# A change to the latent attention stage: values in two 64-column halves, sums in 32-column quarters, a third probability buffer

## Chip, cores and metric

The kernel runs on one core of a Trainium2 chip. The metric is the device time of one launch in microseconds. The kernel is a chain of eight stages (a state-space block, a mixture of experts, a rotary attention, the experts again, the latent attention, a second mixture of experts, a grouped attention, the experts once more); the change touches only the latent attention.

## What is computed

Input `x` is (4, 512, 256). The stage in question adds to `x` the output of `_L1_attn_a_ref` on the layer-normed `x`. Its latent half, cut to what matters:

```
q_mid = rmsnorm(hidden_states @ q_a_w.T, q_a_ln_w)
q = (q_mid @ q_b_w.T).reshape(b, s, H, D_Q).transpose(0, 2, 1, 3)
...
qf = jnp.concatenate([q_nope, q_pe], -1)
kf = jnp.concatenate([k_nope, k_pe], -1)
scores = jnp.einsum('bhqd,bhkd->bhqk', qf, kf) * scale
probs = jax.nn.softmax(scores.astype(jnp.float32), axis=-1).astype(dt)
ctx = jnp.einsum('bhqk,bhkd->bhqd', probs, v)
main_out = ctx.transpose(0, 2, 1, 3).reshape(b, s, H * D_V) @ o_w.T
```

There are 4 batches, 16 heads and 512 tokens. The kernel composes the key and value up-projections with the query and output weights, so that keys and values of all heads are the same 64 latent numbers a token (plus 64 rotary ones for the keys).

## The kernel before

The stage is the function `latent()`. Heads are worked on in 32 pairs (4 batches of 8; `g` counts pairs, `i` is the head within one). A pair has four units, one for each tile of 128 keys (`kt`). One list `events` sets the order of the work, and each engine (PE, ACT, DVE, POOL, and the queue of DMA issues) walks through the same list and takes from it what is its own; a semaphore counter of each engine tells the others how far it is. So the order on an engine is the order of the list, and an instruction that waits holds all that stands behind it on its engine.

In unit `n` the list has: `s` of the first head (three float32r matmuls at L226 to L228 in `mm3` and one that adds the negative maximum, L1932), what `slots` puts at place 0, `s` of the second head, place 1, then `pv` (L1935, probabilities times values) of the unit before for the first head, place 2, `pv` for the second, place 3. A pair has 16 places. The places hold, for the next pair `n`: `kc`, `qc`, `qn` (copies of keys and queries on DVE) at 0, `kp` and `qp` (rope inputs; ACT copies, DMA swaps, POOL combines at L1787, L1789, L1791) at 3 and 11, `mx` (L1921 on PE and the reduction L2128 on DVE) at 4 to 11, `kl` and `ql` (the low halves, L2112) at 5 and 7, `bias` at 13; and for the pair before: `norm` (DVE, L2133 to L2144) at 12, and after every second pair `out` (output projection into DVE's `main`) at 1 and 2. The first pair of a batch has its places otherwise. The side matmuls share two PSUM banks in turn (`slot`), so each waits until the last but one has been read.

The scores of a unit are in two PSUM banks, the exponential (L1987, ACT) writes `PB[n % 2]`, and `pv` reads it as a plain float32 matmul. Its stationary operand is a window of 128 columns of `VT`: 64 columns of values and 64 of ones, the other way round for the second head, so that one matmul gives both the context and the sum of probabilities, head by head in bank 6 and bank 7. `sums` (L1996, L1997, ACT) copies four pieces of 64 partitions, `norm` transposes the sums, takes reciprocals, spreads them and multiplies.

## Time and profile before

| | us |
|---|---|
| time, median of 3 | 4568.15 (4564.28 to 4572.83) |
| profiled execution, its own time | 4568.12 |
| its span | 4566.3 |
| granted TensorE clock, mean | 0.912 |
| PE busy over the span | 3840.6 (84%) |
| DVE busy | 2580.8 (57%) |
| the stage's pairs (1845 to 2730 us) | 885 |

The span runs from the first to the last instruction of the profiled execution. Busy times of engines overlap; which of them sets the end is read from the waits and from the chain of work that ended last. Matmul ends are modelled, so the spacing of starts tells more than durations.

### The profile page before, as it was taken

The numbers are of one execution on the slowest core, as the hardware profiler recorded it, in microseconds if no ns is written. First come the engines' busy times: TensorE is split into PE (matmuls) and PEld (weight loads), VectorE is DVE, ScalarE is ACT, GpSimd is POOL, SyncE is SP. The second block draws the span as 40 slices with busy tenths as digits, with TensorE's granted clock in tenths as the row PEclk, the third lists the DMA queues.
The fourth block names the chain that finished last, engine by engine and source line by source line (L and its number), as shares of the span: only waits on it lengthen the run. The fifth ranks groups of instructions, "written<-read, shape, count | busy, mean of one in ns | idle before, by whom it ended". The sixth has DMA issues, their size and how long they took to land.

```text
span 4566.3 us, 44420 instructions
## 1 busy us (share of the span) xinstructions
PE 3840.6 (84%) x15840; PEld 2548.4 (56%) x15840; DVE 2580.8 (57%) x4324; ACT 1687.5 (37%) x2807; POOL 1353.1 (30%) x1074
## 2 busy tenths in 40 slices
PE   6869778887978883888889887999878888879999
PEld 4647544435844432555555555788744444457887
DVE  5645366654456652678686765433356766655333
ACT  2433256653235540232323223222245555522222
POOL 3234322214320102333323314444322221143442
PEclk8989889988989976999999998999989999979999
DMA  1010000001000002101000101000000000010000
GB/s 56 1 37 5 29 1 1 1 1 41 1 22 5 5 5 80 28 16 26 18 24 17 26 16 58 18 27 9 16 1 1 1 1 1 1 58 21 25 13 19
DMA packets 32760, 83.27 MB, mean 18 GB/s; under 512 B 6304, under 2 KB 7456, under 8 KB 32288
## 3 DMA queue, kind: packets, MB, share of 16 engines
q1 hardware_dynamic: 32544, 80.44, 5.7%
q8 instruction: 130, 2.13, 0.2%
q14 instruction: 86, 0.70, 0.0%
HBM read 59.44 MB, written 4.19 MB: 14 GB/s over the span
## 4 chain that ended last, share of the span: by engine, by line
PE 54%; DVE 22%; ACT 5%; POOL 3%; issue 2%; DMA 1%; SPq 1%; DVEq 0%; POOLq 0%; ACTq 0%
PE ps L226 11%; PE ps L227 10%; PE ps L228 10%; DVE max_cols L1149 7%; PE ps L1096 5%; PE ps L1935 3%; PE ps L1090 2%; PE ps L296 2%; DVE q_lo L2112 2%; DVE max_cols L2128 2%; PE ps L1081 2%; ACT probs L1126 1%; PE ps L1086 1%; PE ps L800 1%; PE ps L1077 1%
## 5 line engine op out<-in xcount | busy, mean ns | idle before, releaser
L1149 DVE TENSOR_REDUCE max_cols<-ps 128x1 fp32r<-128x512 f32 x1024 | 635.6, 680 | 284.9 <-PE ps L1081 284.1
L1126 ACT ACTIVATE probs<-ps 128x512 f32<-128x512 f32 x1024 | 546.1, 603 | 256.5 <-PE ps L1090 164.6
L754 POOL TENSOR_TENSOR h_lo<-h,h_hi 128x512 fp32r<-128x512 f32 x304 | 392.5, 1291 | 816.6 <-ACT h_hi L834 816.6
L911 DVE TENSOR_TENSOR gated<-silu,ps 128x512 f32<-128x512 f32 x288 | 197.9, 687 | 689.1 <-PE ps L228 665.7
L828 ACT ACTIVATE silu<-ps 128x512 f32<-128x512 f32 x304 | 181.9, 598 | 928.0 <-PE ps L228 927.9
L226 PE MATMUL ps<-xn_hi,w_hi 128*128 128x512 f32 x1216 | 479.5, 394 | 0.0
L227 PE MATMUL ps<-xn_lo,w_hi 128*128 128x512 f32 x1216 | 476.0, 391 | 0.0
L228 PE MATMUL ps<-xn_hi,w_lo 128*128 128x512 f32 x1216 | 475.8, 391 | 0.0
L1096 PE MATMUL ps<-probs,v_aug 128*32 128x512 f32 x2048 | 310.3, 683 | 0.0
L330 POOL CAST o_hi<-o_scaled 128x512 fp32r<-128x512 f32 x64 | 39.1, 612 | 910.1 <-DVE o_scaled L1171 910.1
L1935 PE MATMUL ps<-probs,v_tok 128*128 128x512 f32 x512 | 263.5, 611 | 2.7 <-ACT denominators L1997 2.7
L226 PEld LDWEIGHTS ps<-xn_hi,w_hi 128*128 128x128 f32 x1216 | 231.0, 190 | 49.8 <-issue 1.0
L227 PEld LDWEIGHTS ps<-xn_lo,w_hi 128*128 128x128 f32 x1216 | 230.4, 189 | 49.6 <-issue 1.4
L228 PEld LDWEIGHTS ps<-xn_hi,w_lo 128*128 128x128 f32 x1216 | 230.0, 189 | 48.6
L226 PE MATMUL ps<-h_hi,w_hi 128*128 128x512 f32 x608 | 249.4, 410 | 1.2 <-POOL h_lo L754 1.2
L1090 PE MATMUL ps<-q_stack,k_alone 128*128 128x512 f32 x512 | 213.9, 440 | 31.3 <-ACT probs L1126 29.1
L227 PE MATMUL ps<-h_lo,w_hi 128*128 128x512 f32 x608 | 239.7, 394 | 0.0
L228 PE MATMUL ps<-h_hi,w_lo 128*128 128x512 f32 x608 | 239.6, 394 | 0.0
L1090 PE MATMUL ps<-q_stack,k_stack 64*128 64x512 f32 x512 | 198.8, 485 | 43.3 <-ACT probs L1126 41.2
L1987 ACT ACTIVATE probs<-ps 128x1024 f32<-128x1024 f32 x128 | 131.2, 1025 | 279.1 <-PE ps L1932 278.9
L1081 PE MATMUL ps<-k_alone,q_stack 128*128 128x512 f32 x512 | 201.7, 432 | 37.8 <-ACT q_stack L1115 23.7
L2128 DVE TENSOR_REDUCE max_cols<-ps 128x1 fp32r<-128x512 f32 x256 | 169.2, 682 | 89.6 <-PE ps L1921 89.3
(460 smaller groups left out, 7896.1 us busy)
## 6 DMA issues: line engine op xcount, KB each, us to landing
raw<-in_w_ffn SPq DMA_DIRECT2D x76, 448.0 KB, 3.3
raw<-raw SPq DMA_DIRECT2D x256, 64.0 KB, 2.0
composed_inputs<-in_m_latent SPq DMA_DIRECT2D x1, 5120.0 KB, 15.5
raw<-in_w_mamba SPq DMA_DIRECT2D x8, 448.0 KB, 5.9
raw<-in_w_latent SPq DMA_DIRECT2D x5, 448.0 KB, 16.8
x<-in_x SPq DMA_DIRECT2D x4, 512.0 KB, 6.2
gated_pattern<-gated SPq DMA_DIRECT2D x4, 512.0 KB, 3.1
raw<-gated_pattern SPq DMA_DIRECT2D x4, 512.0 KB, 4.3
```

What stands on the lines that cost most here:

```text
L226: nc.tensor.matmul(psum, wh, xh, start=start, stop=False)
L227: nc.tensor.matmul(psum, wh, xl, start=False, stop=False)
L228: return nc.tensor.matmul(psum, wl, xh, start=False, stop=stop)
L754: nc.gpsimd.tensor_tensor(HL[:, b % 3, :], hb[:, b % 2, :], HH[:, b % 3, :].bitcast(F32), ALU.subtract).then_inc(G.sem, G.step((s, ev)))
L911: nc.vector.tensor_tensor(ga if routed(i) else hb[:, i % 2, :], sg[:, i % 2, :], bank[2 + i % 2], ALU.mult).then_inc(V.sem, V.step((s, "ga ...
L1081: last = nc.tensor.matmul(self.psum(ev), self.q_rows(g, h)[:, q * P:(q + 1) * P], self.k_rows(g, h), start=True, stop=True)
L1090: last = nc.tensor.matmul(self.scores(self.step_no(g, kt, h)), self.k_rows(g, h)[:, kt * P:(kt + 1) * P], self.q_rows(g, h), start=True, s ...
L1096: last = nc.tensor.matmul(bank[6][32 * h:32 * h + 32, :], self.VA[:, (g // self.G4) % 2, kt, self.khead((g % self.G4) * 4 + h), :], self.P ...
L1126: nc.scalar.activation(self.PB[:, n % 8, :], self.scores(n), ACT.Exp, scale=self.scale).then_inc(A.sem, A.step((s, ("exp", n))))
L1149: nc.vector.tensor_reduce(self.MB[:, self.tile_of(g, h) % 2, q, col:col + 1], self.psum(ev), op=ALU.max, axis=AX.X, negate=True).then_inc( ...
L1935: last = nc.tensor.matmul(bank[6 + i], VT[:, (g // HP) % 2, kt, 64 - 64 * i:192 - 64 * i], PB[:, (g * QT + kt) % 2, i, :], start=kt == 0, ...
L2128: nc.vector.tensor_reduce(MB[:, q, 32 * i:32 * i + 1], bank[slot(ev)], op=ALU.max, axis=AX.X, negate=True).then_inc(V.sem, V.step((s, ev)))
```

## The change

The values of both heads come out side by side in one bank: two matmuls of 64 columns, into partitions 0 to 63 and 64 to 127 of bank 6. `VT` loses its ones. The sums are matmuls of their own, `add`, after every second key tile: four matmuls with 32 columns of ones, each into 32 partitions of bank 7; a quarter is one head and the even or the odd key tiles. So that both tiles' probabilities are still there, `PB` has three buffers. Both heads' `pv` (and `add`, `sums`) now stand together ahead of places 2 and 3. The copies of `sums` are two of 128 partitions. The transpose of the sums is an event of its own (`turn`, place 7), ACT then swaps neighbouring quarters in four small copies (`swap`, place 10), and `norm` adds the two parts before the reciprocal.

```diff
-            VT = alloc("v_tok", [P, 2, QT, 192])
-            PB = alloc("probs", [P, 2, 2, L])
+            VT = alloc("v_tok", [P, 2, QT, 64])
+            PB = alloc("probs", [P, 3, 2, L])
+            sums = alloc("sums", [P, 2, L // 32])
...
+                put(n, 7, ("turn", g))
+                put(n, 10, ("swap", g))
                 put(n, 12, ("norm", g))
...
-                for i in (0, 1):
-                    if n:
-                        events.append(("pv",) + units[n - 1] + (i,))
-                        if i and units[n - 1][1] == QT - 1:
-                            events.append(("sums", units[n - 1][0]))
-                    events += at[2 + i]
+                if n:
+                    events.append(("pv",) + units[n - 1])
+                    if units[n - 1][1] % 2:
+                        events.append(("add",) + units[n - 1])
+                    if units[n - 1][1] == QT - 1:
+                        events.append(("sums", units[n - 1][0]))
+                events += at[2] + at[3]
...
                     elif kind == "pv":
-                        g, kt, i = ev[1:]
-                        last = nc.tensor.matmul(bank[6 + i], VT[:, (g // HP) % 2, kt, 64 - 64 * i:192 - 64 * i],
-                                                PB[:, (g * QT + kt) % 2, i, :], start=kt == 0, stop=kt == QT - 1)
+                        g, kt = ev[1:]
+                        for i in (0, 1):
+                            last = nc.tensor.matmul(bank[6][64 * i:64 * i + 64, :], VT[:, (g // HP) % 2, kt, :],
+                                                    PB[:, (g * QT + kt) % 3, i, :], start=kt == 0, stop=kt == QT - 1)
+                    elif kind == "add":
+                        g, kt = ev[1:]
+                        for q in range(4):
+                            i, back = q // 2, 1 - q % 2
+                            last = nc.tensor.matmul(bank[7][32 * q:32 * q + 32, :], ones[:, 0:32],
+                                                    PB[:, (g * QT + kt - back) % 3, i, :], start=kt == 1, stop=kt == QT - 1)
...
-                        act.wait_ge(PE.sem, PE.at((s, ("pv", g, QT - 1, 1))))
+                        act.wait_ge(PE.sem, PE.at((s, ("add", g, QT - 1))))
                         if g:
                             act.wait_ge(V.sem, V.at((s, ("norm", g - 1))))
-                        for i in (0, 1):
-                            r, r2 = slice(64 * i, 64 * i + 64), slice(64 - 64 * i, 128 - 64 * i)
-                            nc.scalar.activation(ctx_[r, :], bank[6 + i][r, :], ACT.Copy).then_inc(A.sem, A.step())
-                            nc.scalar.activation(DN[r, :], bank[6 + i][r2, :], ACT.Copy).then_inc(A.sem, A.step((s, ev)))
+                        nc.scalar.activation(ctx_, bank[6], ACT.Copy).then_inc(A.sem, A.step())
+                        nc.scalar.activation(DN, bank[7], ACT.Copy).then_inc(A.sem, A.step((s, ev)))
+                    elif kind == "swap":
+                        act.wait_ge(V.sem, V.at((s, ("turn", ev[1]))))
+                        for q in range(4):
+                            to, of = slice(32 * q, 32 * q + 32), slice(32 * (q ^ 1), 32 * (q ^ 1) + 32)
+                            nc.scalar.activation(sums[to, 0, :], turn_[of, :].rearrange("p (c r) -> p c r", r=32)[:, :, 0],
+                                                 ACT.Copy).then_inc(A.sem, A.step((s, ev)))
...
-                nc.vector.memset(VT[:, :, :, :], 1.0).then_inc(V.sem, V.step())
...
+                    elif kind == "turn":
+                        g = ev[1]
+                        dve.wait_ge(A.sem, A.at((s, ("sums", g))))
+                        if g:
+                            dve.wait_ge(V.sem, V.at((s, ("norm", g - 1))))
+                        nc.vector.transpose(turn_, DN).then_inc(V.sem, V.step((s, ev)))
                     elif kind == "norm":
                         g = ev[1]
-                        dve.wait_ge(A.sem, A.at((s, ("sums", g))))
-                        nc.vector.transpose(turn_, DN).then_inc(V.sem, V.step())
-                        after_last()
-                        nc.vector.reciprocal(few[:, 0, :], turn_.rearrange("p (c r) -> p c r", r=32)[:, :, 0]).then_inc(V.sem, V.step())
+                        dve.wait_ge(A.sem, A.at((s, ("swap", g))))
+                        nc.vector.tensor_tensor(sums[:, 1, :], sums[:, 0, :], turn_.rearrange("p (c r) -> p c r", r=32)[:, :, 0],
+                                                ALU.add).then_inc(V.sem, V.step())
+                        after_last()
+                        nc.vector.reciprocal(few[:, 0, :], sums[:, 1, :]).then_inc(V.sem, V.step())
```

Order on PE in the middle of unit 0 of a pair that follows an output projection's pair, before (`ps<-probs,v_tok` is `pv`, `ps<-o_..,wov_..` the output projection, first for output rows 0 to 127, then for the rest):

```order
L226 MATMUL ps<-o_hi,wov_hi 128x512
L227 MATMUL ps<-o_lo,wov_hi 128x512
L228 MATMUL ps<-o_hi,wov_lo 128x512
L1935 MATMUL ps<-probs,v_tok 128x512
L226 MATMUL ps<-o_hi,wov_hi 128x512
L227 MATMUL ps<-o_lo,wov_hi 128x512
L228 MATMUL ps<-o_hi,wov_lo 128x512
L226 MATMUL ps<-o_hi,wov_hi 128x512
L227 MATMUL ps<-o_lo,wov_hi 128x512
L228 MATMUL ps<-o_hi,wov_lo 128x512
L1935 MATMUL ps<-probs,v_tok 128x512
```

The same place of the change (`ps<-probs,ones` is `add`; the 64 and 32 ahead of the x are the columns of the weights, that is the partitions written):

```order
L226 MATMUL ps<-o_hi,wov_hi 128x512
L227 MATMUL ps<-o_lo,wov_hi 128x512
L228 MATMUL ps<-o_hi,wov_lo 128x512
L1940 MATMUL ps<-probs,v_tok 64x512 x2
L1946 MATMUL ps<-probs,ones 32x512 x4
L226 MATMUL ps<-o_hi,wov_hi 128x512
L227 MATMUL ps<-o_lo,wov_hi 128x512
L228 MATMUL ps<-o_hi,wov_lo 128x512
L226 MATMUL ps<-o_hi,wov_hi 128x512
L227 MATMUL ps<-o_lo,wov_hi 128x512
L228 MATMUL ps<-o_hi,wov_lo 128x512
```

The second head's values have moved ahead of the second output projection, and four sum matmuls with them.

Order on DVE over the maxima (`max_cols`) and the start of `norm` in an ordinary pair, before:

```order
L2128 TENSOR_REDUCE max_cols<-ps 128x1 x2
L2112 TENSOR_TENSOR k_lo<-raw,k_hi 64x512 x2
L2128 TENSOR_REDUCE max_cols<-ps 128x1 x2
L2112 TENSOR_TENSOR q_lo<-raw,q_hi 64x512 x2
L2128 TENSOR_REDUCE max_cols<-ps 128x1 x4
L2133 STREAM_TRANSPOSE raw<-denominators 128x512
L2135 RECIPROCAL few<-raw 128x16
```

And of the change:

```order
L2142 TENSOR_REDUCE max_cols<-ps 128x1 x2
L2126 TENSOR_TENSOR k_lo<-raw,k_hi 64x512 x2
L2142 TENSOR_REDUCE max_cols<-ps 128x1
L2149 STREAM_TRANSPOSE raw<-denominators 128x512
L2142 TENSOR_REDUCE max_cols<-ps 128x1
L2126 TENSOR_TENSOR q_lo<-raw,q_hi 64x512 x2
L2142 TENSOR_REDUCE max_cols<-ps 128x1 x4
L2153 TENSOR_TENSOR sums<-sums,raw 128x16
L2156 RECIPROCAL few<-sums 128x16
```

The transpose has moved from behind the eighth maximum to between the third and the fourth, and an addition has come in ahead of the reciprocal.

## Rows read from the trace of the kernel before

**Rows 1.** The page's part 4: chain that ended last, share of the span.

```profile
PE 54%; DVE 22%; ACT 5%; POOL 3%; issue 2%; DMA 1%; SPq 1%; DVEq 0%; POOLq 0%; ACTq 0%
PE ps L226 11%; PE ps L227 10%; PE ps L228 10%; DVE max_cols L1149 7%; PE ps L1096 5%; PE ps L1935 3%; PE ps L1090 2%; PE ps L296 2%; DVE q_lo L2112 2%; DVE max_cols L2128 2%; PE ps L1081 2%; ACT probs L1126 1%; PE ps L1086 1%; PE ps L800 1
```

**Rows 2.** Windows: busy time by engine, PEclk; latent pairs, then an attention stage.

```profile
1845.00:2730.00 885.00, 778.93 (x2767) 518.44 (x2766) 647.53 (x937) 287.35 (x388) 259.71 (x204) 0.96 0.08 21
1340.00:1680.00 340.00, 288.55 (x1396) 145.26 (x1394) 216.41 (x364) 181.82 (x339) 36.74 (x34) 0.91 0.01 5
```

**Rows 3.** Groups of instructions, 1845 to 2730: count, busy us, mean ns, idle before.

```profile
L1935 PE MATMUL ps<-probs,v_tok 128*128 128x512 f32 x512 | 263.5, 611 | 2.7 <-ACT denominators L1997 2.7
...
L1997 ACT ACTIVATE denominators<-ps 64x512 f32<-64x512 f32 x64 | 38.0, 593 | 1.6
...
L1980 ACT ACTIVATE raw<-ps 128x512 f32<-128x512 f32 x60 | 35.9, 599 | 157.4 <-PE ps L228 152.8 <-POOL raw L1791 3.9
...
L2135 DVE RECIPROCAL few<-raw 128x16 f32<-128x16 f32 x32 | 8.1, 253 | 1.1
...
L1963 ACT ACTIVATE roots<-sq,eps_rms 128x16 f32<-128x16 f32 x6 | 1.6, 314 | 8.4 <-DVE sq L2062 8.4
```

**Rows 4.** Waits of PE, 1845 to 2730: us in total, times, longest.

```profile
PE ps L1921 <- DVE max_cols L2128: 62.9, 32, 4.2
PE ps L226 <- DVE q_lo L2123: 23.0, 11, 4.0
...
PE ps L1935 <- ACT denominators L1997: 2.7, 4, 0.7
```

**Rows 5.** Timeline, maxima of one pair: start us, us, engine, line, operation.

```profile
2104.20 0.39 PE L1921 MATMUL ps<-k_hi,q_hi 128*128 128x512 f32 x1
...
2109.10 1.09 POOL L1789 TENSOR_TENSOR raw<-raw,c 128x512 f32<-128x512 f32 x1
2109.14 3.27 DVE L2112 TENSOR_TENSOR q_lo<-raw,q_hi 64x512 fp32r<-64x512 f32 x2
...
2110.28 1.59 POOL L1791 TENSOR_TENSOR raw<-raw 128x512 f32<-128x512 f32 x1
...
2113.07 0.50 PE L1921 MATMUL ps<-k_hi,q_hi 128*128 128x512 f32 x1 [1.97 <-DVE max_cols L2128]
...
2114.49 0.39 PE L226 MATMUL ps<-qmid_hi,w_latent_hi 128*128 128x512 f32 x1
```

**Rows 6.** Timeline of PE around one full-width float32 matmul.

```profile
2008.67 1.02 PE L1935 MATMUL ps<-probs,v_tok 128*128 128x512 f32 x2
...
2009.76 0.39 PE L227 MATMUL ps<-xn_lo,w_latent_hi 128*128 128x512 f32 x1
2009.99 0.40 PE L228 MATMUL ps<-xn_hi,w_latent_lo 128*128 128x512 f32 x1
```

**Rows 7.** Timeline of PE: sixteen 64-column matmuls at the stage's start.

```profile
1767.85 4.93 PE L1833 MATMUL ps<-composed_inputs 128*64 128x256 f32 x32
```

**Rows 8.** Timeline of PE around groups of four 32-column float32 matmuls.

```profile
1500.30 1.07 PE L1096 MATMUL ps<-probs,v_aug 128*32 128x512 f32 x8
1501.30 0.50 PE L226 MATMUL ps<-xn_hi,w_pattern_hi 128*128 128x512 f32 x1
1501.64 0.40 PE L227 MATMUL ps<-xn_lo,w_pattern_hi 128*128 128x512 f32 x1
...
3363.70 0.39 PE L228 MATMUL ps<-xn_hi,w_grouped_lo 128*128 128x512 f32 x1
3364.02 1.07 PE L1096 MATMUL ps<-probs,v_aug 128*32 128x512 f32 x8
```

**Rows 9.** Timeline of PE: second output projection behind its wait, short and long.

```profile
2099.53 0.50 PE L226 MATMUL ps<-o_hi,wov_hi 128*128 128x512 f32 x1 [1.28 <-DVE q_lo L2123]
...
2152.68 0.78 PE L226 MATMUL ps<-o_hi,wov_hi 128*128 128x512 f32 x1 [3.70 <-DVE q_lo L2123]
```

**Rows 10.** One line's instructions: duration in ns min/median/max.

```profile
L2133 DVE STREAM_TRANSPOSE raw<-denominators x32: 700/702/712, 1889.0 to 2724.6; 128x512 f32<-128x512 f32 x32
```

More of the change, by code:

```diff
@@ L1736, in latent @@
                     events += at[i]
-                for i in (0, 1):
-                    if n:
-                        events.append(("pv",) + units[n - 1] + (i,))
-                        if i and units[n - 1][1] == QT - 1:
-                            events.append(("sums", units[n - 1][0]))
-                    events += at[2 + i]
-            events += [("norm", PAIRS - 1), ("out", PAIRS // 2 - 1, 0), ("out", PAIRS // 2 - 1, 1), ("tail", NB - 1)]
+                if n:
[5 more added lines that the diff above has]
+                events += at[2] + at[3]
+            events += [("turn", PAIRS - 1), ("swap", PAIRS - 1), ("norm", PAIRS - 1), ("out", PAIRS // 2 - 1, 0), ("out", PAIRS // 2 - 1, 1), ("tail", NB - 1)]
             reader = {"mean": V, "var": V, "mid": A, "power": V, "tokens": A, "gate": V, "kp": A, "qp": A, "qn": V, "mx": V,
@@ L1933, in pe @@
                     elif kind == "pv":
-                        g, kt, i = ev[1:]
-                        last = nc.tensor.matmul(bank[6 + i], VT[:, (g // HP) % 2, kt, 64 - 64 * i:192 - 64 * i],
-                                                PB[:, (g * QT + kt) % 2, i, :], start=kt == 0, stop=kt == QT - 1)
+                        g, kt = ev[1:]
[3 more added lines that the diff above has]
+                    elif kind == "add":
+                        g, kt = ev[1:]
+                        for q in range(4):
+                            i, back = q // 2, 1 - q % 2
+                            last = nc.tensor.matmul(bank[7][32 * q:32 * q + 32, :], ones[:, 0:32],
+                                                    PB[:, (g * QT + kt - back) % 3, i, :], start=kt == 1, stop=kt == QT - 1)
                     elif kind == "out":
@@ L1967, in act @@
                         act.wait_ge(PE.sem, PE.at((s, ev)))
-                        nc.scalar.activation(VT[:, b % 2, :, 64:128], bank[slot(ev)].rearrange("p (q d) -> p q d", d=P)[:, :, 0:64],
+                        nc.scalar.activation(VT[:, b % 2, :, :], bank[slot(ev)].rearrange("p (q d) -> p q d", d=P)[:, :, 0:64],
                                              ACT.Copy).then_inc(A.sem, A.step((s, ev)))
@@ L1986, in act @@
                         act.wait_ge(PE.sem, PE.at((s, ev)))
-                        nc.scalar.activation(PB[:, n % 2, :, :], ps[n % 2][:, :, :], ACT.Exp,
+                        nc.scalar.activation(PB[:, n % 3, :, :], ps[n % 2][:, :, :], ACT.Exp,
                                              scale=AQ ** -0.5).then_inc(A.sem, A.step((s, ("exp", n))))
```

## Prediction

> **What bounds the kernel now.** I read the page first: the chain that ended last is 54% TensorE (PE) and 22% VectorE (DVE), and the line that is changed, L1935, has 3% of the span in it [rows 1]. The change lies in one stage, so the next view is the windows of that stage: 885 us of a span of 4566.3, in which PE is busy 779, DVE 648 and ScalarE (ACT) 287, at a granted clock of 0.96 [rows 2]. In the groups of that stage L1935, the matmuls of probabilities by values, is the costliest: 512 records, two to a float32 matmul, for 256 matmuls [rows 3]. The waits say who ends PE's idle time: L1921 waits for the maxima on DVE 62.9 us in 32 waits, and the output projection waits for q_lo L2123 23.0 us in 11 waits; ACT's sums hold L1935 only four times [rows 4].
>
> The timeline shows why. A pair of heads has four units (key tiles 0 to 3). In a typical pair (some 24 of the 32, read one by one) the eight maxima matmuls L1921 stand in units 1 and 2. From 2104.20 to 2109.84 PE is not held. Then k_lo on DVE has released GpSimd's (POOL) rope chain; POOL's L1789 and L1791 and DVE's two q_lo subtractions take turns, and the two q_lo take 3.27 us. Only then are maxima reduced, and PE restarts at 2113.07 after 1.97 us idle and leaves the phase at 2114.49 [rows 5]. So units 1 and 2 end on DVE and POOL, units 3 and 0 on PE, except where the output projection (unit 0, every second pair) waits for q_lo of the queries.
>
> **What a tile of columns costs.** Before, one full-width float32 matmul takes 0.86 us: L1935 starts at 2008.67, the next but one matmul at 2009.76, which is 1.09 less one ordinary spacing of 0.23 [rows 6]. Both heads: 1.71 us a unit, 128 x 1.71 = 219 us in the stage.
> The trace has no 64-column matmul with 512 moving columns. It has two near ones. L1833 (64 columns, 256 moving, sixteen matmuls) takes 4.93 us in all, though its first half runs before the clock rises; one after the other at full clock would be 16 x 0.43 = 6.9 us, so the two halves run together [rows 7]. L1096 is four 32-column float32 matmuls by 512, just the form of the new sums: start to next start 1.00, and the next matmul's own spacing is 0.34 instead of 0.23; on entry the spacing before it is 0.32 instead of 0.23 [rows 8]. One excursion of four is thus 1.00 + 0.11 + 0.09 = 1.20 us where the two overlapped slots are 0.86: about 0.33 us is the price of leaving the full width and coming back.
> I take 1.19 for the two 64-column matmuls, since the four of [rows 8] have as many weight columns in all. For values and sums together I take 2 x 0.86 + 0.33 + 0.16 for the turn from 64 to 32 columns (half an excursion): 2.20 us. That turn is between 0 and 0.33.
> So on PE alone two units cost 3.39 after against 3.43 before. What the narrow matmuls win is nearly taken back by the sums and by the switching. The Trainium skill (TensorEngine Tiling, Key Properties) says that changing the tiling mode drains TensorE; [rows 8] agree with it, with the 0.33 above. Without such a price two units would cost 2.57, and 64 x 0.86 = 55 us of PE work would go.
>
> **The change unit by unit.**
> Unit 3 (values alone, PE ends it): 1.71 to 1.19 is -0.52. In 28 pairs -14.6 us; in the four where the next output projection waits 3 us or more (as at 2152.68 [rows 9]) the wait swallows it.
> Unit 0 (values and sums of the pair before): +0.49 in the 21 pairs without a wait: +10.3 us. In the 11 with one [rows 4, 9] the whole group now stands ahead of the second projection, so PE works 2.20 us in place of 0.86 before the wait, and owes nothing behind it. The short waits, like 1.28 at 2099.53, vanish: 1.71 + 1.28 - 2.20 = -0.8; the long ones end when q_lo ends, and the second head's 0.86 behind them is gone. 11 x -0.83 = -9 us.
> Units 1 and 2: PE's work in unit 2 rises to 2.20 ahead of the seventh L1921, but it waits 1.97 there anyway. What matters is DVE. The transpose of the denominators (0.70 us [rows 10]) now stands between the third and fourth maximum, ahead of q_lo, as the rows of order ahead show. By [rows 5]: q_lo could start at 2109.14; it now starts 0.70 later, at 2109.84, still inside POOL's L1789, which ends at 2110.19. So the first q_lo gets its turn at the same time as before; L1791 has its turn until 2111.87, and the second q_lo ends 0.54 behind it at 2112.41, as before. The later start is swallowed by the queue with POOL. Then three reductions as before; the matmul behind the last L1921 (2114.49 before [rows 5]) needs the seventh maximum's bank, which comes free near 2114.4. About -0.1 in 24 pairs, -3 us. Bounds: -0.4, if the reductions close up, and +0.7, if all of the transpose shows. All transposes took 0.700 to 0.712, POOL busy or not, so I take the transpose as no party to the turns [rows 10].
> The addition of the two quarters (128x16; nearest the reciprocal, 0.25 [rows 3]) and its wait are 8 us of DVE in unit 3, where DVE has slack and norm loses the 0.70: nothing. Behind it are the next pair's copies, which gain 0.4.
> ACT: four 64-partition copies (0.59 each [rows 3]) become two of 128 partitions (the 128x512 copy is 0.60 [rows 3]): the sums are out 1.2 us sooner after a group that ends 0.49 later. That shows where L1935 waited for them, four times: -3 us. The four swaps of 32x16 are new; the nearest row is the 128x16 square root of 0.31 [rows 3], which I take for each. They wait for the transpose behind the third maximum, stand on ACT after unit 2's exponential, and behind them is only the copy for the next rope, ahead of which ACT sat idle 157 us over 60 copies [rows 3]. Nothing; uncovered they would be 32 x 1.2 = 38 us.
> The last pair's tail is serial: +0.5 for the sums, -1.2 for ACT, +1.2 swaps, +0.3: +1 us. The third probability buffer lets the exponential run while sums wait, and keeps ACT off PE: nothing. The memset of values goes, in a start that waits for loads: nothing.
> Sum: -14.6 + 10.3 - 9 - 3 - 3 + 1 = **-18 us**. The sum is made against the profiled execution, whose own time 4568.12 (span 4566.3 and 1.8 around it) equals the median 4568.15. Forecast 4550.
>
> **The rivals.** About 9 us (0.2%) is what a measurement of this kernel can tell from no change.
> (a) As above: 4550, range 4540 to 4559. Chance 0.5.
> (b) Switching is cheap for 64 columns or is hidden (its own price is not in the trace). Unit 3 -0.86, unit 0 none in 21 pairs and -0.86 in 11: -24 - 9 - 5 = -38, 4530. For it: L1833 shows no gap when steady. Against it: the 0.33 of [rows 8]. Chance 0.12. The Trainium skill (TensorE: Matmul & The Clock Gate, Part 3) has the span of packed tiles as one matmul plus some 4 ns for each further tile, which is this case; by it the price of an excursion would be near nothing, as here. What [rows 8] show is 0.33 us more where full-width work stands on both sides.
> (c) DVE is later: the transpose shows in full in the maxima phase of 24 pairs, +0.7 each, 17 us, and eats the gain: 4567, no change. For it: that phase ends on DVE in each pair; against it the turns with POOL reckoned above. 0.2.
> (d) Slower: PE's clock. The stage is granted 0.96 on the mean, near the level of 2.4 GHz; behind the long wait at 2152.68 the first matmul takes 0.78, behind the short one at 2099.53 0.50 [rows 9]: the long wait took PE to the lower clock level. If the narrow matmuls or the chopped waits bring more such stretches and the mean falls to 0.92 (a stage with many 32-column groups and waits has 0.91 [rows 2]), 0.04 of 885 us is +35: 4585. It decides from a clock of 0.94 on. Against it: the long waits get shorter by 0.5 to 1.3 us. 0.12.
> (e) Slower: the two 64-column matmuls of 512 do not run together. Then unit 3 is +0.33 and unit 0 +1.35: 9 + 28 - 6 = +31, 4599. It decides once a pair costs 0.3 more than I take. Against it [rows 7]. 0.06.
>
> **How the numbers follow.** The predicted time is (a)'s, 4550. Leaving out the last two cases and little of (b) gives 4528 to 4574; (a) alone is 4540 to 4559. Faster by over 0.2%: nearly all of (a), (b), a little of (c): 0.62. Within 0.2%: most of (c), the edge of (a): 0.2. Slower: (d), (e): 0.18.
>
> **What would show it.** In the trace after: the group of two 64-column matmuls with 1.1 to 1.3 us from entry to exit, values and sums 2.0 to 2.4; PE's 11 waits for q_lo L2123's successor from 23 us to 10 or less; first L1921 to the matmul behind the last still near 10.3 us, q_lo still 3.27 or 2.7; the transpose 0.70; stage 885 to about 867, clock 0.96. Wrong it would be by a 64-to-32 turn above 0.33, a q_lo that ends later, or a clock under 0.95.

## Result and the profile after

The changed kernel took 4554.83 us (median of 20 runs) beside 4567.54 for the kernel before: ratio 0.9973, 95% interval 0.9964 to 0.9982, so 12.7 us less, between 8 and 16. A second set on another chip (last experiment) gave 0.9984 (0.9971 to 0.9997). The forecast was 18 us less, 4550, with a range from 4528 to 4574. The range held; the 18 us lie just outside the interval.

The profiled execution took 4549.46 us. A large part of its 18.7 us below the one before has nothing to do with the change: the attention stage ahead of this one took 384.3 us before and 375.9 after from its first L1081 matmul to its last L1096, with the same code, and 368 to 382 in the other profiles. So from here on a kernel is judged by the stretch of its own stage from the first maxima matmul of the first pair to that of the last (below: the stage). It went from 855.9 to 847.8 us, 8.1 less, and a second profile of the changed kernel gave 847.7. The timed 8 to 16 us less agree with it.

The page's part 4 (the chain of work that ended last) and then the window over that stretch (busy us of PE, weight loads, DVE, ACT and POOL, then the granted clock), which answer to [rows 1, 2]:

```profile
PE 53%; DVE 23%; ACT 5%; POOL 3%; issue 2%; DMA 1%; SPq 0%; DVEq 0%; POOLq 0%; ACTq 0%
```

```profile
1821.10:2668.90 847.80, 763.05 (x3157) 446.73 (x3157) 633.05 (x947) 264.77 (x430) 266.22 (x207) 0.96 0.09 22
```

The kernel before had 755.05 us of TensorE (PE) busy in its 855.90: PE is no less busy for the narrow matmuls. e1 below, the full-width kernel in the new order, has 763.3 too. The groups (count, busy us, mean ns, idle before), answering to [rows 3, 10]:

```profile
L1940 PE MATMUL ps<-probs,v_tok 128*64 128x512 f32 x512 | 139.2, 622 | 0.1
...
L1946 PE MATMUL ps<-probs,ones 128*32 128x512 f32 x512 | 68.2, 605 | 0.0
...
L2011 ACT ACTIVATE sums<-raw 32x16 f32<-32x16 f32 x128 | 29.0, 227 | 3.9 <-DVE raw L2149 0.8
```

```profile
L2149 DVE STREAM_TRANSPOSE raw<-denominators x32: 682/694/712, 1869.9 to 2701.6; 128x512 f32<-128x512 f32 x32
```

PE's waits in the stage (us in total, times, longest), answering to [rows 4]:

```profile
PE ps L1925 <- DVE max_cols L2142: 45.1, 53, 4.0
PE ps L226 <- DVE q_lo L2137: 12.7, 8, 2.9
PE ps L226 <- DVE max_cols L2142: 6.3, 27, 0.5
PE ps L226 <- ACT max_rows L1994: 5.9, 19, 0.9
```

The wait of the output projection fell from 23.0 in 11 to 12.7 in 8. Four of the seven short waits, which the forecast let vanish, are still there with 0.42 to 0.68 us. The last row is new in size: before there were 2.9 us in four such waits.

Timeline of PE, one group of values and sums (start us, us), answering to [rows 6, 8]:

```profile
2059.25 1.08 PE L1940 MATMUL ps<-probs,v_tok 128*64 128x512 f32 x4
2060.26 1.07 PE L1946 MATMUL ps<-probs,ones 128*32 128x512 f32 x8
2061.25 0.50 PE L226 MATMUL ps<-xn_hi,w_latent_hi 128*128 128x512 f32 x1
2061.59 0.39 PE L227 MATMUL ps<-xn_lo,w_latent_hi 128*128 128x512 f32 x1
```

From 2059.25 to 2061.25 are 2.00, and with 0.09 on entry and 0.11 on leaving 2.20: the number in the forecast. So the prices of the narrow matmuls are not where it went wrong.

Timeline of a pair's maxima, answering to [rows 5]:

```profile
2114.76 0.39 PE L1925 MATMUL ps<-k_hi,q_hi 128*128 128x512 f32 x1
...
2118.99 0.69 DVE L2149 STREAM_TRANSPOSE raw<-denominators 128x512 f32<-128x512 f32 x1
...
2120.29 2.69 DVE L2126 TENSOR_TENSOR q_lo<-raw,q_hi 64x512 fp32r<-64x512 f32 x2
...
2120.83 1.60 POOL L1795 TENSOR_TENSOR raw<-raw 128x512 f32<-128x512 f32 x1
...
2122.91 2.56 DVE L2142 TENSOR_REDUCE max_cols<-ps 128x1 fp32r<-128x512 f32 x4
```

The two q_lo start later but take 2.69 instead of 3.27, and end as late after the first maxima matmul as before (8.22 and 8.21 us). The transpose in front of them costs nothing, as forecast: the second q_lo ends 0.55 us behind POOL's last operation, as before (0.54). From the first to the last maxima matmul, start to start (below: the maxima phase), an ordinary pair takes 9.47 us instead of 9.66; e1 has 9.47 too, so this comes with the order.

To see where 8.1 us come from, each unit is timed from the first record of the value group that stands in it to that of the next (the start columns of the timeline, 128 groups). That stretch ends later than the stage as defined above, so the sums differ a little from its length. Sums over the stage, and in brackets an ordinary pair:

| us | before | e1, order alone | changed |
|---|---|---|---|
| unit 0 | 227.6 (5.41) | 216.7 (5.41) | 224.8 (5.89) |
| unit 1 | 152.2 (4.49) | 152.7 (4.49) | 152.1 (4.51) |
| unit 2 | 275.4 (8.04) | 273.3 (8.03) | 278.3 (8.00) |
| unit 3 | 208.8 (6.42) | 208.5 (6.42) | 199.2 (6.12) |
| all | 864.0 | 851.2 | 854.4 |

### The profile page after: what moved, and what is told of

Read it like the earlier page. It is cut to its first block, busy times and chain, and to the rows that moved or that the text cites. A ratio compares the mean times of both kernels' runs of the same rounds, so it can differ in the third digit from the quotient of the medians.

```text
span 4547.7 us, 45570 instructions
## 1 busy us (share of the span) xinstructions
PE 3830.8 (84%) x16352; PEld 2483.2 (55%) x16352; DVE 2576.8 (57%) x4355; ACT 1675.3 (37%) x2871; POOL 1356.0 (30%) x1074
## 4 chain that ended last, share of the span: by engine, by line
PE 53%; DVE 23%; ACT 5%; POOL 3%; issue 2%; DMA 1%; SPq 0%; DVEq 0%; POOLq 0%; ACTq 0%
PE ps L226 11%; PE ps L228 10%; PE ps L227 10%; DVE max_cols L1149 7%; PE ps L1096 4%; DVE max_cols L2142 3%; PE ps L1090 2%; PE ps L296 2%; PE ps L1081 2%; DVE q_lo L2126 2%; ACT probs L1126 1%; PE ps L1086 1%; PE ps L800 1%; PE ps L1940 1%; PE ps L1077 1%
## 5 line engine op out<-in xcount | busy, mean ns | idle before, releaser
L1149 DVE TENSOR_REDUCE max_cols<-ps 128x1 fp32r<-128x512 f32 x1024 | 635.9, 680 | 285.6 <-PE ps L1081 284.9
L226 PE MATMUL ps<-xn_hi,w_hi 128*128 128x512 f32 x1216 | 479.4, 394 | 0.0
L228 PE MATMUL ps<-xn_hi,w_lo 128*128 128x512 f32 x1216 | 475.6, 391 | 0.0
L1096 PE MATMUL ps<-probs,v_aug 128*32 128x512 f32 x2048 | 302.1, 665 | 0.0
L226 PEld LDWEIGHTS ps<-xn_hi,w_hi 128*128 128x128 f32 x1216 | 230.7, 190 | 49.4 <-issue 1.0
L228 PEld LDWEIGHTS ps<-xn_hi,w_lo 128*128 128x128 f32 x1216 | 230.2, 189 | 48.6
L226 PE MATMUL ps<-h_hi,w_hi 128*128 128x512 f32 x608 | 248.9, 409 | 1.2 <-POOL h_lo L754 1.2
L228 PE MATMUL ps<-h_hi,w_lo 128*128 128x512 f32 x608 | 239.3, 394 | 0.0
L1081 PE MATMUL ps<-k_alone,q_stack 128*128 128x512 f32 x512 | 202.1, 431 | 38.6 <-ACT q_stack L1115 23.8
L1791 POOL TENSOR_TENSOR raw<-raw,c 128x512 f32<-128x512 f32 x64 | 75.0, 1172 | 480.8 <-DVE k_lo L2126 291.3
L1081 PE MATMUL ps<-k_stack,q_stack 64*128 64x512 f32 x512 | 177.5, 457 | 35.9 <-DVE q_stack L1155 12.9
## 6 DMA issues: line engine op xcount, KB each, us to landing
raw<-in_w_latent SPq DMA_DIRECT2D x5, 448.0 KB, 16.9
```

The costliest lines, as they stand in the source:

```text
L226: nc.tensor.matmul(psum, wh, xh, start=start, stop=False)
L228: return nc.tensor.matmul(psum, wl, xh, start=False, stop=stop)
L1081: last = nc.tensor.matmul(self.psum(ev), self.q_rows(g, h)[:, q * P:(q + 1) * P], self.k_rows(g, h), start=True, stop=True)
L1096: last = nc.tensor.matmul(bank[6][32 * h:32 * h + 32, :], self.VA[:, (g // self.G4) % 2, kt, self.khead((g % self.G4) * 4 + h), :], self.P ...
L1149: nc.vector.tensor_reduce(self.MB[:, self.tile_of(g, h) % 2, q, col:col + 1], self.psum(ev), op=ALU.max, axis=AX.X, negate=True).then_inc( ...
```

## Experiments

All in one table first. "Stage" is the stretch defined above, from one profiled execution each; "q_lo" is PE's wait for q_lo at the second output projection; PEclk is the granted clock of the stage; "slow" counts the L226 to L228 matmuls (of 1527) whose successor starts 0.40 to 0.46 us later instead of 0.23, that is, at the lower clock level.

| kernel | ratio to before (95%) | stage us | q_lo us, times | PEclk | slow |
|---|---|---|---|---|---|
| before | 1 | 855.9 | 23.0, 11 | 0.96 | 69 |
| changed | 0.9973 (0.9964 to 0.9982) | 847.8 | 12.7, 8 | 0.96 | 86 |
| e1 order alone, full width | 0.9966 (0.9951 to 0.9981) | 844.6 | 13.2, 10 | 0.96 | 86 |
| e2 bias sooner | 0.9990 (0.9974 to 1.0007) | 848.4 | 17.9, 10 | 0.97 | 74 |
| e3 transpose late | 1.0015 (1.0001 to 1.0029) | 862.1 | 16.9, 10 | 0.95 | 98 |
| e4 sums of tiles 0, 1 only | 0.9956 (0.9940 to 0.9972) | 836.1 | 25.4, 14 | 0.95 | 94 |
| e5 group late in unit 0 | 1.0035 (1.0019 to 1.0050) | 871.6 | 32.7, 11 | 0.96 | 72 |
| e6 changed, q first | 0.9929 (0.9909 to 0.9948) | 819.1 | none | 0.97 | 41 |
| e7 e1, q first | 0.9943 (0.9920 to 0.9967) | 823.6 | none | 0.97 | 71 |
| e8 sums of tiles 2, 3 only | 0.9997 (0.9982 to 1.0012) | 857.1 | 11.2, 9 | 0.93 | 148 |
| e9 before, q first | 0.9944 (0.9924 to 0.9963) | 835.3 | none | 0.95 | 88 |
| e10 changed, both edits | 0.9917 (0.9900 to 0.9933) | 816.7 | none | 0.98 | 34 |
| e11 e4, q first | 0.9848 (0.9829 to 0.9868) | 794.2 | none | 0.98 | 46 |
| e12 changed again | 0.9984 (0.9971 to 0.9997) | 847.7 | 12.7, 8 | 0.96 | 86 |

**Which part of the change brings the gain.** e1 is the kernel before with the order alone:

```diff
                 for i in (0, 1):
                     if n:
                         events.append(("pv",) + units[n - 1] + (i,))
                         if i and units[n - 1][1] == QT - 1:
                             events.append(("sums", units[n - 1][0]))
-                    events += at[2 + i]
+                events += at[2] + at[3]
```

> The kernel before with only the order changed: both value matmuls of a unit stand together, ahead of both halves of the unit's other work; they keep their full width, and the sums stay in them. Theory (the gain comes from the 11 output projections that wait for q_lo on VectorE, since the whole group now stands ahead of the second projection): 11 x 0.86 = 9.5 us less than before, 4558, with TensorE's waits for q_lo from 23 us to about 13, and nothing in the pairs without a projection. Rival (the narrow matmuls themselves bring the gain, the order is neutral): 4567, waits for q_lo near 23 us.

Measured: 0.9966, stage 11.3 us less than before. Moving one value matmul a unit ahead of the work at place 2 gives what the whole change gives; with the 64-column matmuls, the separate sums, the swaps and the third buffer added, the stage is 3.2 us longer (854.4 against 851.2 in the table of units), which one profile of each hardly tells from nothing. e5 is the counterpart, the changed kernel with unit 0's group behind the second projection:

```diff
+                late = n and units[n - 1][1] == QT - 1
+                if late:
+                    events += at[2]
                 if n:
                     events.append(("pv",) + units[n - 1])
...
-                events += at[2] + at[3]
+                events += ([] if late else at[2]) + at[3]
```

> The changed kernel, narrow matmuls and all, with the group of values and sums in unit 0 behind the second output projection instead of ahead of it; units 1 to 3 as in the changed kernel. Theory (the gain of the change is the cover that the group gives to that projection's wait, and the narrow matmuls bring nothing): TensorE's waits for q_lo go from 12.7 us back to 23 or more, unit 0 is 1 to 2 us longer in some 11 pairs, and the time is 12 to 18 us over the changed kernel's: 4567 to 4573, the time before or above. Rival (the narrow matmuls bring the gain, the place is neutral): 4555.

Measured: slower than before, 1.0035, stage +23.8 on the changed kernel, waits for q_lo 32.7: more than expected (12 to 18), since the whole 2.20 us group now follows the wait. That the place brings the gain holds.

**The loss in unit 3.** In the changed kernel ScalarE (ACT) holds PE at a pair's end. Timeline of PE and then of ACT, where pair 2 ends and pair 3 begins:

```profile
1903.90 1.08 PE L1940 MATMUL ps<-probs,v_tok 128*64 128x512 f32 x4
1905.17 0.50 PE L226 MATMUL ps<-q_hi,k_hi 128*128 128x512 f32 x1 [0.20 <-ACT max_rows L1994]
```

```profile
1903.61 1.03 ACT L1998 ACTIVATE probs<-ps 128x1024 f32<-128x1024 f32 x1 [1.16 <-PE ps L1936]
1904.53 0.59 ACT L1994 ACTIVATE max_rows<-ps 128x512 fp32r<-128x512 f32 x1
```

The exponential of unit 3 and behind it the copy of the maxima's rows take 1.5 us; a full-width value group covered them, the narrow one does not. e2 puts the copy ahead of the exponential:

```diff
-                    put(g, 13, ("bias", n))
+                    put(g, 12, ("bias", n))
```

> The changed kernel with one event moved: the ordinary pairs' bias matmul, and with it ScalarE's copy of the maxima's rows, stands one place sooner, ahead of the exponential of unit 3. Theory (unit 3's 0.52 us per pair are lost because the shortened value group no longer covers the exponential, 1.02, and the copy, 0.6, on ScalarE): the 19 waits of L226 for that copy (5.9 us, and 21.1 us of the weight load) nearly vanish, non-output pairs go from 24.40 to about 24.2, and the time is 5 to 8 us under the changed kernel's: about 4548. Rival (the price of leaving and re-entering full width is larger in unit 3 than reckoned): the waits vanish and the time stays at 4555. Second rival (the exponential is now late for the next value group): waits of L1940 for the probabilities appear and the time rises, 4560.

Measured: all but four of the waits vanish (2.7 us are left), unit 3 falls from 6.12 to 5.86 (199.2 to 195.2 in all), and the stage gains nothing: 848.4. No gain came, as the first rival had it, but not by its reason, since unit 3 did get shorter. Unit 0 took it back, from 224.8 to 230.2, nearly all of it in the eleven units whose projection had waited in the kernel before; their waits for q_lo rose from 12.7 to 17.9 us. That made a new theory: on the pairs with a projection something other than PE sets the time, and what PE saves in the unit before comes back as wait. e2 alone is weak evidence for it. Of the 5.2 us, 3.6 are in pairs 3 and 21, where POOL's second product waited for its DMA swap longer than in the changed kernel, 4.37 us for 2.46 and 4.16 for 2.70 (timeline of POOL, pair 3 of e2):

```profile
1916.49 1.09 POOL L1793 TENSOR_TENSOR raw<-raw,c 128x512 f32<-128x512 f32 x1 [4.37 <-DMA raw<-raw]
```

e10 below has both swaps late again, so it may belong to this order; why was not tried. The other projections' waits rose by 1.6 us in all, which the theory can claim. e4 puts it to a stronger test. It leaves out the sums of key tiles 2 and 3, the group in unit 0:

```diff
-                    if units[n - 1][1] % 2:
+                    if units[n - 1][1] == 1:
...
-                        act.wait_ge(PE.sem, PE.at((s, ("add", g, QT - 1))))
+                        act.wait_ge(PE.sem, PE.at((s, ("pv", g, QT - 1))))
```

> The changed kernel with the second of a pair's two groups of 32-column sums left out: the denominators hold key tiles 0 and 1 alone, and what stands in unit 0 of the next pair is the values group alone. It measures what the sums in unit 0 cost. Theory (unit 0 ends on TensorE in the 21 pairs that don't wait, and the group adds 2.20 - 1.19 = 1.0 us there): 21 x 1.0 = 21 us under the changed kernel, 4534, and a few more where the group stands ahead of a wait. Rival (unit 0's work is hidden behind other engines too): 4550 or more.

Measured: ordinary pairs get shorter by exactly the 1.0 (5.89 to 4.90), but the long-wait pairs get longer by 0.9 to 1.2 us (11.53 to 12.45 and 12.75), waits for q_lo go from 12.7 to 25.4, and of 21 us reckoned 11.7 are seen in the stage. In pair 3 the wait rises by the 1.0 us left out, from 2.60 to 3.59, and behind it eleven matmuls are slow instead of seven: that is why the pair gets longer and not merely no shorter. The theory stands on this run.

**What sets those pairs.** Timeline of the changed kernel, the same pair 3, VectorE (DVE), GpSimd (POOL) and PE:

```profile
1906.34 1.09 POOL L1793 TENSOR_TENSOR raw<-raw,c 128x512 f32<-128x512 f32 x1 [2.46 <-DMA raw<-raw]
1907.51 1.29 POOL L1795 TENSOR_TENSOR raw<-raw 128x512 f32<-128x512 f32 x1
...
1908.76 2.37 POOL L1814 TENSOR_TENSOR x<-x,raw 128x1024 f32<-128x1024 f32 x1
1908.84 3.03 DVE L2119 CAST q_hi<-raw 64x512 fp32r<-64x512 f32 x2 [3.51 <-POOL raw L1795]
...
1911.80 1.40 DVE L2133 CAST q_hi<-ps 64x512 fp32r<-64x512 f32 x2
...
1913.23 1.41 DVE L2137 TENSOR_TENSOR q_lo<-ps,q_hi 64x512 fp32r<-64x512 f32 x2
...
1914.70 0.50 PE L226 MATMUL ps<-o_hi,wov_hi 128*128 128x512 f32 x1 [2.60 <-DVE q_lo L2137]
```

DVE stands idle 3.51 us for POOL's rope of the query (which itself waited 2.46 us for the DMA that swaps its input), then casts it while POOL is at work (3.03 for two), and only then reads the projected query out of the PSUM bank that the second projection needs. PE's last matmul for it had begun at 1907.38. POOL's L1814, once a batch, stands in pairs 3, 11, 19 and 27; these are the four long waits. e6 exchanges the two on DVE and touches no other engine's order:

```diff
-                    put(g, 0, ("kc", n), ("qc", n), ("qn", n))
+                    put(g, 0, ("kc", n), ("qn", n), ("qc", n))
```

> The changed kernel with one exchange on VectorE: the cast and subtraction of the projected query (from PSUM, whose bank the second output projection waits for) stand ahead of the cast of the roped query, which waits for GpSimd. The order of every other engine is the same. Theory (the long waits of unit 0 hang on the GpSimd rope chain and on the casts that take turns with GpSimd's next add, 3.0 us for two, and that is where TensorE's savings in other units were given back): the 12.7 us of waits for q_lo vanish and unit 0 of the output pairs goes to about 7.2 to 8.9 us: 10 to 15 us less than the changed kernel, about 4542. Rival (the wait only moves, to the maxima matmuls in units 1 and 2, which then wait for q_hi): no gain, 4555.

The same place in e6:

```profile
1914.69 1.41 DVE L2133 CAST q_hi<-ps 64x512 fp32r<-64x512 f32 x2 [2.45 <-PE ps L228]
1916.13 1.41 DVE L2137 TENSOR_TENSOR q_lo<-ps,q_hi 64x512 fp32r<-64x512 f32 x2
1917.46 1.29 DVE L2119 CAST q_hi<-raw 64x512 fp32r<-64x512 f32 x2
```

```profile
1917.92 1.07 PE L1946 MATMUL ps<-probs,ones 128*32 128x512 f32 x8
1918.91 0.50 PE L226 MATMUL ps<-o_hi,wov_hi 128*128 128x512 f32 x1
```

Measured: 0.9929 against 0.9973, some 20 us, and by the stage 28.7, twice what was expected. Unit 0 of the eleven pairs is 7.28 or 7.29 (11.53 to 11.80 in the long-wait pairs of the changed kernel). Gone are the 12.7 us of waits, 4.5 more in which two maxima matmuls waited for q_lo, and 45 slow matmuls, 9 us at 0.20 each: 26 of the 28.7. Of the slow ones 27 had stood behind the four long waits; the rest of the fall is in units 2 and 3, 1.4 us of it in pair 15, so part of the gain came with the clock and not with the wait itself. Behind the long wait of pair 3 the first matmuls from 1914.70 on are 0.34, 0.23, 0.29, 0.43 and 0.43 apart. Nothing of it reappears in the maxima phase, 9.47 us in both.

e7 and e9 put the same exchange into the full-width kernel of e1 and into the kernel before.

> The full-width kernel with both value matmuls together (the first experiment) and the same exchange on VectorE as in the run beside it. Theory (full width and narrow cost TensorE the same over two units, and unit 0 ends on TensorE, so the narrow kernel pays 0.49 there in each pair and wins 0.3 to 0.57 in unit 3): the two kernels agree within 5 us, both near 4542. Rival (with the wait for q_lo gone TensorE bounds the output pairs, and the narrow matmuls' shorter unit 3 now counts): the narrow one is 5 to 10 us under the full-width one.

> The kernel before, unchanged but for the exchange on VectorE (the projected query's cast and subtraction ahead of the roped query's cast). Theory (all that the change gained was cover for the wait of the second output projection for q_lo; with that wait gone at its source the change has nothing left to give): the 23.0 us of waits vanish, the time falls by 20 to 30 us to about 4540, and the stage from first to last maxima matmul is within 5 us of the two kernels with the same exchange (819 narrow, 824 full width together). Rival (standing together is worth something of its own, by one excursion or one wait less in unit 2): this kernel stays 10 us or more above them.

Measured, by the stage: 835.3 (before), 823.6 (together, full width), 819.1 (narrow). The exchange alone is worth 20.6 us in the kernel before. By unit that is 33.2 less in unit 0, of which unit 2 takes 17.6 back. The theory that the change has nothing left to give then is wrong by the stage: 11.7 us for standing together remain, all in unit 2 (293.0 against 279.9), where ten units take 9.6 to 9.7 instead of 8.0 in e9 and six in e7. The narrow matmuls take off another 4.5, which is inside what a few slow stretches do. The timed ratios (0.9944, 0.9943, 0.9929) don't separate the three, so this stands on one profile of each.

e10 and e11 repeat e2 and e4 with the exchange in place.

> The changed kernel with both edits: the exchange on VectorE, and the ordinary pairs' bias matmul one place sooner (the second experiment, which took the wait for ScalarE out of unit 3 and gained nothing). Theory (that gain was given back as wait for q_lo in the next output pair; with those waits gone it counts): unit 3 goes from 6.12 to 5.86 in 16 pairs and unit 0 does not rise, so the stage is 3 to 5 us under 819, about 815, and the time near 4529. Rival (it is given back elsewhere again, in the maxima phase): 819 and 4533.

> The changed kernel with the exchange on VectorE and the second group of sums left out (denominators hold key tiles 0 and 1 alone), to be read against the fourth experiment, where leaving the same group out gave 13 us and not the 21 that unit 0 was reckoned at. Theory (what was missing had been given back as wait for q_lo): now every pair's unit 0 is 1.0 us shorter, 31 x 1.0, and the stage goes from 819 to about 788 to 792. Rival (VectorE bounds a pair as soon as TensorE gets shorter): 800 or more, with longer waits for max_cols.

Measured: e10's stage is 2.5 us under e6 (unit 3 5.5 less, unit 2 2.8 more, unit 0 1.5 more, all in pair 3 with its late swap), ratio 0.9917, the lowest of a kernel that leaves nothing out: 4532.5 us beside 4566.1 before. Its interval overlaps that of e6 (0.9929), so the edit of e2 is not shown to gain even here. e11's stage is 24.9 under e6, where the same omission had given 11.7. Savings on PE count once the wait for q_lo is gone; by e11 the theory holds, with 2 to 6 us less than reckoned.

**The transpose's place.** e3 moves transpose and swaps back to place 12:

```diff
-                put(n, 7, ("turn", g))
-                put(n, 10, ("swap", g))
+                put(n, 12, ("turn", g))
+                put(n, 12, ("swap", g))
```

> The changed kernel with the transpose of the denominators and the four swaps moved back from the maxima phase (places 7 and 10) to place 12, where the transpose stood before, ahead of the reciprocal. Theory (the 0.70 us of transpose is swallowed by the turns that q_lo takes with GpSimd): maxima phase the same within 0.1 us, and at place 12 the chain transpose, swaps, addition (0.7 + 1.0 + 0.2) sits on ScalarE ahead of the exponential or the maxima's copy, so 0 to +10 us: 4555 to 4565. Rival (the transpose shows in the maxima phase of 24 pairs): 0.3 to 0.7 us off each of those phases, 4540 to 4548.

Measured: slower, stage +14.3. The ordinary maxima phase is 9.47 with the transpose in it and without it: it is swallowed, and rival (c) of the forecast is out. The price is elsewhere, more than the 0 to 10 us expected. In the three pairs at a batch's border, whose units 1 to 3 have some 10 us of it, the phase goes from 9.1 to 9.2 up to 11.64, since DVE stands there 2.26 us for the swaps and PE 3.24 for DVE:

```profile
2053.89 0.19 DVE L2153 TENSOR_TENSOR sums<-sums,raw 128x16 f32<-128x16 f32 x1 [2.26 <-ACT sums L2011]
```

**The sums in unit 2.** e8 leaves out the other group (key tiles 0 and 1):

```diff
-                    if units[n - 1][1] % 2:
+                    if units[n - 1][1] == 3:
```

> The changed kernel with the first of a pair's two groups of sums left out (the one in unit 2): the denominators hold key tiles 2 and 3 alone. Theory (the 1.0 us of sums in unit 2 stands ahead of the seventh maxima matmul, which waits for VectorE anyway, 0.8 to 1.0 us): unit 2 stays at 8.0 in the ordinary pairs, and the time is 0 to 4 us under the changed kernel's. Rival (the sums delay the maxima matmul and with it VectorE): unit 2 is 0.3 to 1.0 us shorter and the time 8 to 24 us less.

Measured: less work and 9.3 us more in the stage, which neither the theory nor the rival had. Timeline of PE, pair 10, changed kernel and then e8:

```profile
2123.64 1.09 PE L1925 MATMUL ps<-k_hi,q_hi 128*128 128x512 f32 x2 [0.83 <-DVE max_cols L2142]
2124.92 0.50 PE L226 MATMUL ps<-qmid_hi,w_latent_hi 128*128 128x512 f32 x1 [0.19 <-DVE max_cols L2142]
2125.26 0.39 PE L227 MATMUL ps<-qmid_lo,w_latent_hi 128*128 128x512 f32 x1
2125.49 0.40 PE L228 MATMUL ps<-qmid_hi,w_latent_lo 128*128 128x512 f32 x1
```

```profile
2142.13 1.39 PE L1925 MATMUL ps<-k_hi,q_hi 128*128 128x512 f32 x2 [1.81 <-DVE max_cols L2142]
2143.70 0.80 PE L226 MATMUL ps<-qmid_hi,w_latent_hi 128*128 128x512 f32 x1 [0.18 <-DVE max_cols L2142]
2144.30 0.63 PE L227 MATMUL ps<-qmid_lo,w_latent_hi 128*128 128x512 f32 x1
2144.72 0.63 PE L228 MATMUL ps<-qmid_hi,w_latent_lo 128*128 128x512 f32 x1
```

The wait grows from 0.83 to 1.81, the omitted 1.0 us: that much the theory had. But the matmuls behind it then start 0.42 apart instead of 0.23, eleven of them, at a granted clock of 0.50 (2143.70 to 2147.50). This unit takes 10.71 instead of 8.01. Slow matmuls rise from 86 to 148, and the granted clock falls from 0.96 to 0.93. That is rival (d) of the forecast, with a wait of 1.8 us and in a kernel that does less.

**Repeatability.** e12 is the changed kernel unedited.

> The changed kernel once more, beside the others on their chip, for how far one profiled execution of it stands for the next. Theory: the units of the stage repeat to 0.02 us where no half-clock stretch lies, the stage within 3 us of 847.8, and the ratio to the kernel before again 0.9973 within 0.0015.

Measured: stage 847.7, unit sums within 0.4 us of the first profile. Other kernels were profiled once each, so a difference of some 3 us between two of them is not settled by this.

## Why the prediction came out as it did

**Sign, range and the gain of the order: right.** The wait of the second projection and what moves ahead of it were reckoned at 11 x -0.83 = -9. Those eleven units went from 108.2 to 99.8 us, -8.5, and e1 and e5 show that it is the order that does it. The waits themselves fell only to 12.7 us, not to the 10 or less of the forecast.

**Prices of the narrow matmuls: right.** Values and sums 2.20, values alone 1.19 with entry and exit (unit 3 of pair 9, which nothing holds, fell from 6.41 to 5.84), unit 0 +0.48 for +0.49. For values and sums together there was luck in it: the 0.16 for a turn from 64 to 32 columns was an assumption, the turn shows no price, and the groups themselves take as much more. Rivals (b) and (e) are out.

**Unit 0 without a wait: over-counted.** Forecast 21 x 0.49 = +10.3, measured +5.7. Sixteen units pay 0.3 to 0.5; in the last pair of each batch the unit gets 0.35 to 0.37 shorter. This error offset most of the next.

**The step that failed: "Unit 3 (values alone, PE ends it): 1.71 to 1.19 is -0.52. In 28 pairs -14.6 us".** The stage has -9.6 in unit 3. "PE ends it" was read off a trace in which the full-width group covered what other engines do beneath it. In eleven ordinary pairs it covered ACT's exponential and copy; with the cover gone they gain 0.30 and not 0.57, and e2 shows it, getting back 4.0. In pairs 7, 15 and 23, the last of their batches, it covered DVE's last maxima (PE's waits of the bias matmul, before and after):

```profile
PE ps L1925 <- DVE max_cols L2128: 1.2, 3, 0.4
...
PE ps L1929 <- DVE max_cols L2142: 3.4, 3, 1.1
```

These pairs took 6.99 or 7.00 us each before and take 6.99, 8.44 and 8.41 after, 4.4 us over the forecast together, which is more than the eleven pairs lose. In the two that got longer the first seven full-size matmuls behind the wait run at a granted clock of 0.50 (2280.90 to 2284.00), in pair 7 the same ones at 1.00 (2055.80 to 2059.00). That is rival (d) in small.

The step had a second fault: it let the next projection's wait swallow the gain in four pairs, where e4 shows a saving ahead of such a wait given back at each of the eleven (waits for q_lo 12.7 to 25.4).

**Units 1 and 2, and ACT's sums: -3 and -3 forecast, +2.8 and nothing found.** PE's waits for ACT's sums did vanish, but unit 1, where they stood, is 152.1 against 152.2. Ordinary unit 2 fell by 0.04; the pairs in a batch's middle, with a wait of 3 us for DVE and slow matmuls behind it, rose (the three with 10.2 to 11.1 us to 11.5). Single pairs differ by more, in both directions (pairs 10 and 24 together 2.8 up, 21, 26 and 28 together 5.0 down), with where slow matmuls fall. e1, with full-width matmuls, has 273.3 there, so the rise goes with the narrow ones as far as one profile of each can say; which of their edits does it was not separated.

**Sum.** Forecast for the stage -19 without the tail, measured -8.1 (-9.6 by the table of units: -8.5, +5.7, -9.6 in unit 3, +2.9 and -0.1). The range held because these errors stayed small and partly offset each other. Split by e1: the order gives -11.3, the narrow matmuls with all they need +3.2. The forecast had given them about as much as the order, -10.

**What it missed altogether** is that the wait for q_lo, 23.0 us in its own rows, had a removable cause. It was priced for how much of it the change covers; one exchange on DVE takes away all of it, 20.6 us in the kernel before, after what unit 2 takes back in slow matmuls.

## What to carry to other kernels

When a wait is covered by moved work, ask first what the waited-for engine was doing: here DVE sat 3.51 us for data that the waiting engine did not need. "PE ends this unit" holds only at the old lengths; before a group is shortened, add up what the other engines do beneath it. And where an engine waits regularly for another, a saving ahead of the wait is worth little and may cost (the long-wait pairs of e4, unit 2 of e8), while once the wait is gone the same saving is worth most of its size (e11).

## What the runs showed of the hardware

**Less work, slower clock.** The same wait of 1.81 us that is followed by eleven matmuls at the lower level in pair 10 of e8 (granted clock 0.50) is followed by full speed in its pair 18 (1.00 from 2369.80 to 2373.00), with the same instructions in the unit. There the projection behind the two maxima matmuls starts 1.29 after the first of them (1.28 in the changed kernel), and not 1.57:

```profile
2368.48 1.09 PE L1925 MATMUL ps<-k_hi,q_hi 128*128 128x512 f32 x2 [1.81 <-DVE max_cols L2142]
2369.77 0.50 PE L226 MATMUL ps<-qmid_hi,w_latent_hi 128*128 128x512 f32 x1 [0.19 <-DVE max_cols L2142]
```

Both profiles of the changed kernel have 86 slow matmuls, so it may be something that the kernel's own course decides and not chance; what decides it wasn't tried.

**DVE was slowed beside POOL where it read SBUF, not where it read PSUM.** The cast of a query from SBUF took 3.03 us for two halves while POOL added 128x1024 (until 1911.13, the casts until 1911.87), 1.29 mostly past it in e6, and 0.88 with POOL idle (at 2044.76 in e3); the same cast from PSUM took 1.41 right beside POOL's L1795 (at 1914.69 in e6), and 1.40 with POOL idle (at 1911.80). The Trainium skill (SBUF — State Buffer, SBUF: two separate sides) has VectorE and GpSimd share one pair of ports, held for a whole instruction, by VectorE operations in a two-port mode or with two SBUF inputs (the latter only against a GpSimd operation that reads SBUF). These rows agree with it; that the cast from SBUF ran in such a mode no run here shows.

**Going to narrow columns and back cost 0.2 us beyond the matmuls, at both widths:** 0.09 on entry, 0.11 on leaving, at 64 as at 32 columns [rows 8], and the turn from 64 to 32 columns, for which the forecast took 0.16, shows no price of its own: 2.00 for both groups, where either alone takes 1.01 or 1.00. What the forecast had put on the turn, the groups themselves take (1.00 each and not 0.86), so its sum came out right.
